# A modulated linear layer as the first stage of a long kernel, rebuilt as a pipeline over batches

## The reference

```
# first operation, per batch b (y = cond_1024, 8 x 256; weight 256 x 256)
w = scale * weight[:, :, :, 0] * y[:, None, :]
dnorm = rsqrt(sum(w * w, axis=2, keepdims=True) + 1e-08)
w = w * dnorm
E = Efou.reshape(b, in_f, img_size)
x = einsum('boi,bil->bol', w, E).reshape(b, img_size, out_f)
# second operation, the part concerned
qkv = x @ qkv_w
q_l = q.reshape(b, h, m, l, dh).mean(axis=3)      # m = 64 landmarks of l = 8 tokens
k_l = k.reshape(b, h, m, l, dh).mean(axis=3)
attn2 = softmax(q_l @ k_l^T) ; attn2_inv = six Newton iterations (pseudo-inverse)
```

## Time and profile before

| | us |
|---|---|
| median of the runs | 4001.85 |
| profiled execution, its own time | 3965.16 |
| its span, first to last instruction | 3963.4 |
| first matmul of `nystrom_stage` in it | 82.63 |
| mean granted TensorE clock | 0.746 of full |
| busy share: PE, DVE, ACT, POOL | 83%, 57%, 43%, 30% |

### The profile page before, as it was taken

The page is one execution under the profiler, slowest core; times in us unless marked ns, Lnnn a source line. Parts: engine busy times, 40 slices in busy tenths (PEclk is TensorE's granted clock), DMA queues, the critical chain, the costliest instruction groups (busy, mean ns, idle before and its releaser), DMA issues. The chain is left out here.

```text
span 3963.4 us, 142208 instructions
## 1 busy us (share of the span) xinstructions
PE 3296.6 (83%) x58228; PEld 2450.2 (62%) x58228; DVE 2267.9 (57%) x6676; ACT 1694.8 (43%) x5249; POOL 1201.1 (30%) x1587
## 2 busy tenths in 40 slices
PE   5667759898888888559984899999999979999682
PEld 4455448888888888535531466666666647777561
DVE  4437754444444444368865777877779755555333
ACT  0129633333333333247742455655556534444231
POOL 0012330000000000023320555554555554444432
PEclk8789955555555555589997899999999975555686
DMA  3001010000000000011101000000000010101335
GB/s 119 8 26 54 19 42 24 14 14 24 14 24 14 24 14 24 5 33 24 24 0 49 2 2 2 2 2 2 2 2 2 2 45 31 35 31 35 87 118 170
DMA packets 111064, 115.69 MB, mean 29 GB/s; under 512 B 53132, under 2 KB 94549, under 8 KB 110458
## 3 DMA queue, kind: packets, MB, share of 16 engines
q1 hardware_dynamic: 102762, 87.07, 7.8%
q0 software_dynamic: 7824, 21.46, 1.5%
HBM read 79.49 MB, written 29.00 MB: 27 GB/s over the span
## 5 line engine op out<-in xcount | busy, mean ns | idle before, releaser
L649 PE MATMUL banks<-hp,whp 128*128 128x8 f16 x24576 | 741.3, 168 | 117.5 <-DVE hp L716 117.5
L649 PEld LDWEIGHTS banks<-hp,whp 128*128 128x128 f16 x24576 | 697.7, 104 | 178.3 <-DVE hp L716 169.4
L682 ACT ACTIVATE ig<-banks 128x32 f32<-128x32 f32 x512 | 101.2, 198 | 577.5 <-PE banks L649 577.5
L1043 ACT ACTIVATE att_PH<-att_stp 128x1024 f16<-128x1024 f32 (+3 forms) x258 | 183.4, 711 | 374.0 <-PE att_stp L861 374.0
L711 DVE SCALAR_TENSOR_TENSOR carry<-ig 128x16 f32<-128x16 f32 x512 | 92.2, 180 | 425.3 <-ACT ig L682 425.3
L619 POOL COPY HT<-hist 128x128 f32 x64 | 21.2, 406 | 986.6 <-DVE hp L721 986.6
L1659 PEld LDWEIGHTS rnn_banks<-rnn_hp,rnn_whp 128*128 128x128 f16 x6144 | 251.8, 108 | 102.3 <-ACT rnn_hp L1717 70.9
L1659 PE MATMUL rnn_banks<-rnn_hp,rnn_whp 128*128 128x8 f16 x6144 | 285.5, 171 | 35.3 <-ACT rnn_hp L1717 11.2
L1108 POOL TENSOR_TENSOR att_QK<-att_rot,att_QK 128x512 f16<-128x512 f32 x133 | 173.6, 1305 | 338.5 <-ACT att_QK L1035 338.5
L627 PE MATMUL banks<-xs,wxp 128*128 128x64 f16 x3168 | 264.9, 241 | 0.0
L979 DVE TENSOR_TENSOR att_PL<-att_P,att_PH 128x1024 f16<-128x1024 f32 (+3 forms) x257 | 235.1, 934 | 18.1 <-ACT att_P L1049 16.5
(11 more groups left out here) (572 smaller groups left out, 7910.8 us busy)
## 6 DMA issues: line engine op xcount, KB each, us to landing
gen_w<-in_L_cond_W_dram SPq DMA_DIRECT2D x32, 512.0 KB, 4.2
exp_xt<-expert_rows_scratch SPq DMA_DIRECT2D x80, 129.0 KB, 2.3
edge_cb<-cols_scratch SPq DMA_DIRECT2D x16, 512.0 KB, 3.7
XT<-expert_found_scratch SPq DMA_DIRECT2D x16, 512.0 KB, 5.1
mod_xn<-in_x_dram SPq DMA_DIRECT2D x8, 512.0 KB, 3.7
XT<-in_xT_dram SPq DMA_DIRECT2D x1, 4096.0 KB
out_dram<-exp_ob SPq DMA_DIRECT2D x64, 64.0 KB, 2.2
attw_st<-in_L_attn_w_qkvT_dram SPq DMA_DIRECT2D x6, 512.0 KB, 4.4
```

What stands on the lines that cost most here:

```text
L649: last=nc.tensor.matmul(out, whp[:,wpart,k,col:col+128], hp[:,k,hpart], start=False,stop=True,skip_group_check=True)
L1043: nc.scalar.activation(PH[:,:,at:at+w_],st_ps[:,:,0:w_],ACT.Exp,scale=DH**-0.5)
```

## The change

`dense_stage` gets four buffers for `xn`, three for `wy`, and two for `sq`, `ps_n`, `rt` and `dn`. Scaling and squaring move from VectorE to ScalarE (`Copy` with a scale, and `Square`), one batch ahead of the root. TensorE sums the squares of batch b+1 before it mixes batch b. VectorE takes the reciprocal of batch b, then sums the eight-token groups of batch b-1 (`landmarks`, two instructions of 512 columns), then writes `HT` of batch b. SyncE issues `XT` after the attention's weights instead of ahead of them. `nystrom_stage` loses its two long sums and TensorE's wait for them; `lm` is allocated outside of both stages, and the counts of the semaphore `dv` shift by one.

```diff
-def dense_stage(nc, XT, HT, x, xT, condT, wT_in, h0T, loads):
+def dense_stage(nc, XT, HT, x, xT, condT, wT_in, h0T, lm, loads):
 
     with ExitStack() as ctx:
         sb=lambda n,s,d=F32: ctx.enter_context(nc.sbuf_tensor("mod_"+n,s,d))
         sem=ctx.enter_context(semaphores(nc,"mod_"))
-        W=sb("W",[P,2,D]); xn=sb("xn",[P,2,2,2*D]); wy=sb("wy",[P,2,2,D]); sq=sb("sq",[P,2,D]); rt=sb("rt",[P,D]); dn=sb("dn",[P,D]); eps=sb("eps",[P,1]); ones=sb("ones",[P,P]); ysc=sb("ysc",[P,2,NB])
-        ps_n=ctx.enter_context(nc.psum_tensor("mod_ps_n",[P,512],F32)); ps_d=ctx.enter_context(nc.psum_tensor("mod_ps_d",[P,2,2,512],F32))
-        x_in=[sem(f"x_in{i}") for i in range(2)]; w_in,h_in,xt_in,rest_in,const,yscaled,modded,squared,summed,rooted,inverted,mixed,kept=[sem(n) for n in "w_in,h_in,xt_in,rest_in,const,yscaled,modded,squared,summed,rooted,inverted,mixed,kept".split(",")]
+        XB=4; WB=3
+        W=sb("W",[P,2,D]); xn=sb("xn",[P,XB,2,2*D]); wy=sb("wy",[P,WB,2,D]); sq=sb("sq",[P,2,2,D]); rt=sb("rt",[P,2,D]); dn=sb("dn",[P,2,D]); eps=sb("eps",[P,1]); ones=sb("ones",[P,P]); ysc=sb("ysc",[P,2,NB])
+        ps_n=ctx.enter_context(nc.psum_tensor("mod_ps_n",[P,2,512],F32)); ps_d=ctx.enter_context(nc.psum_tensor("mod_ps_d",[P,2,2,512],F32))
+        x_in=[sem(f"x_in{i}") for i in range(XB)]; w_in,h_in,xt_in,rest_in,const,yscaled,modded,squared,summed,rooted,inverted,mixed,kept,meaned=[sem(n) for n in "w_in,h_in,xt_in,rest_in,const,yscaled,modded,squared,summed,rooted,inverted,mixed,kept,meaned".split(",")]
         block=ctx.enter_context(nc.Block())
         @block.sync
         def _(sp):
@@ -71,10 +72,10 @@
             sp.dma_start(h0T[:,:,:],condT).then_inc(h_in,16)
             sp.dma_start(W[:,:,:],wT_in.rearrange("(k p) o -> p k o",p=P)).then_inc(w_in,16)
             for b in range(NB):
-                if b>=2: sp.wait_ge(mixed,b-1)
-                sp.dma_start(xn[:,b%2],x[b].rearrange("(k i h) f -> i k (h f)",k=2,h=2)).then_inc(x_in[b%2],16)
+                if b>=XB: sp.wait_ge(mixed,b-XB+1)
+                sp.dma_start(xn[:,b%XB],x[b].rearrange("(k i h) f -> i k (h f)",k=2,h=2)).then_inc(x_in[b%XB],16)
+            for dst,src in loads: sp.dma_start(dst,src).then_inc(rest_in,16)
             sp.dma_start(XT[:,:,:,:],xT).then_inc(xt_in,16)
-            for dst,src in loads: sp.dma_start(dst,src).then_inc(rest_in,16)
             sp.wait_ge(xt_in,16); sp.wait_ge(rest_in,16*len(loads))
         @block.gpsimd
         def _(pool):
@@ -82,45 +83,58 @@
             nc.gpsimd.memset(eps[:,:],1e-8).then_inc(const,1)
         @block.vector
         def _(dve):
-            dve.wait_ge(h_in,16); dve.wait_ge(w_in,16)
+            dve.wait_ge(h_in,16)
             nc.vector.tensor_scalar(ysc[:,:,:],h0T[:,:,:],D**-0.5,None,ALU.mult).then_inc(yscaled,1)
-            dve.wait_ge(yscaled,1)
+            def landmarks(b):
+                dve.wait_ge(kept,b+1)
+                for k in range(2): i=nc.vector.tensor_reduce(out=lm[:,k,b*LMK:(b+1)*LMK],in_=HT[:,k,b,:].rearrange("p (m g) -> p m g",g=GROUP),axis=X_AX,op=ALU.add)
+                i.then_inc(meaned,1)
             for b in range(NB):
-                if b>=2: dve.wait_ge(mixed,b-1)
-                for k in range(2): nc.vector.tensor_scalar(wy[:,b%2,k],W[:,k],ysc[:,k,b:b+1],None,ALU.mult).then_inc(modded,1)
-                dve.wait_ge(modded,2*b+2); dve.wait_ge(summed,b)
-                nc.vector.tensor_tensor(sq[:,:,:],wy[:,b%2],wy[:,b%2],ALU.mult).then_inc(squared,1)
                 dve.wait_ge(rooted,b+1)
-                nc.vector.reciprocal(dn[:,:],rt[:,:]).then_inc(inverted,1)
+                if b>=2: dve.wait_ge(kept,b-1)
+                nc.vector.reciprocal(dn[:,b%2],rt[:,b%2]).then_inc(inverted,1)
+                if b: landmarks(b-1)
                 dve.wait_ge(mixed,b+1); dve.wait_ge(inverted,b+1)
                 for k in range(2):
                     for h in range(2):
-                        i=nc.vector.tensor_tensor(HT[:,k,b,h:T:2],ps_d[:,b%2,k,h*D:(h+1)*D],dn[:,:],ALU.mult)
+                        i=nc.vector.tensor_tensor(HT[:,k,b,h:T:2],ps_d[:,b%2,k,h*D:(h+1)*D],dn[:,b%2],ALU.mult)
                 i.then_inc(kept,1)
+            landmarks(NB-1)
         @block.scalar
         def _(act):
-            act.wait_ge(const,2)
+            act.wait_ge(const,2); act.wait_ge(yscaled,1); act.wait_ge(w_in,16)
+            def modulate(b):
+                if b>=WB: act.wait_ge(mixed,b-WB+1)
+                for k in range(2): nc.scalar.activation(wy[:,b%WB,k],W[:,k],ACT.Copy,scale=ysc[:,k,b:b+1]).then_inc(modded,1)
+                act.wait_ge(modded,2*b+2)
+                if b>=2: act.wait_ge(summed,b-1)
+                nc.scalar.activation(sq[:,b%2],wy[:,b%WB],ACT.Square).then_inc(squared,1)
+            modulate(0)
             for b in range(NB):
+                if b+1<NB: modulate(b+1)
                 act.wait_ge(summed,b+1)
-                if b: act.wait_ge(inverted,b)
-                nc.scalar.activation(rt[:,:],ps_n[:,0:D],ACT.Sqrt,bias=eps[:,0:1]).then_inc(rooted,1)
+                if b>=2: act.wait_ge(inverted,b-1)
+                nc.scalar.activation(rt[:,b%2],ps_n[:,b%2,0:D],ACT.Sqrt,bias=eps[:,0:1]).then_inc(rooted,1)
         @block.tensor
         def _(pe):
             pe.wait_ge(const,2)
+            def sums(b):
+                pe.wait_ge(squared,b+1)
+                if b>=2: pe.wait_ge(rooted,b-1)
+                for k in range(2): i=nc.tensor.matmul(ps_n[:,b%2,0:D],ones[:,:],sq[:,b%2,k],start=(k==0),stop=(k==1))
+                i.then_inc(summed,1)
+            sums(0)
             for b in range(NB):
-                pe.wait_ge(squared,b+1)
-                if b: pe.wait_ge(rooted,b)
-                for k in range(2): i=nc.tensor.matmul(ps_n[:,0:D],ones[:,:],sq[:,k],start=(k==0),stop=(k==1))
-                i.then_inc(summed,1)
-                pe.wait_ge(x_in[b%2],16*(b//2+1))
+                if b+1<NB: sums(b+1)
+                pe.wait_ge(x_in[b%XB],16*(b//XB+1))
                 if b>=2: pe.wait_ge(kept,b-1)
                 for f in range(2):
                     for h in range(2):
-                        for k in range(2): i=nc.tensor.matmul(ps_d[:,b%2,f,h*D:(h+1)*D],xn[:,b%2,k,h*D+f*P:h*D+(f+1)*P],wy[:,b%2,k],start=(k==0),stop=(k==1))
+                        for k in range(2): i=nc.tensor.matmul(ps_d[:,b%2,f,h*D:(h+1)*D],xn[:,b%XB,k,h*D+f*P:h*D+(f+1)*P],wy[:,b%WB,k],start=(k==0),stop=(k==1))
                 i.then_inc(mixed,1)
 
 
...
-def nystrom_stage(nc, HT, wqkv, out_w, out_b, conv, xg, ident, taps_dram):
+def nystrom_stage(nc, HT, lm, wqkv, out_w, out_b, conv, xg, ident, taps_dram):
...
-            lm=sb1("mean",[P,2,NB*LMK]); qbd=sb1("qbd",[P,LP,NB,P]); kl=sb1("kl",[P,LP,NB*LMK]); klbd=sb1("klbd",[P,LP,P])
+            qbd=sb1("qbd",[P,LP,NB,P]); kl=sb1("kl",[P,LP,NB*LMK]); klbd=sb1("klbd",[P,LP,P])
...
-                for k in range(2): i=nc.vector.tensor_reduce(out=lm[:,k,:],in_=HT[:,k,:,:].rearrange("p b (m g) -> p (b m) g",g=GROUP),axis=X_AX,op=ALU.add)
-                step(i)
...
-                pe.wait_ge(dv,1)
                 proj(A,0,[lm[:,k,:] for k in range(2)])
...
-            wqkv=sb0("lm_wqkv",[P,2,3*LI]); out_w=sb0("lm_out_w",[P,LP,D]); out_b=sb0("lm_out_b",[P,2]); xg=sb0("xg",[P,2,T])
+            wqkv=sb0("lm_wqkv",[P,2,3*LI]); out_w=sb0("lm_out_w",[P,LP,D]); out_b=sb0("lm_out_b",[P,2]); xg=sb0("xg",[P,2,T]); lm=sb0("lm_mean",[P,2,NB*LMK])
```

More of the change, by code:

```diff
@@ L220, in _ @@
                 nc.scalar.activation(v[:,:,:],A[:,:,:],ACT.Copy).then_inc(ac,1)
-                act.wait_ge(dv,5)
+                act.wait_ge(dv,4)
                 nc.scalar.activation(A2[:,:,:],A2[:,:,:],ACT.Exp).then_inc(ac,1)
-                act.wait_ge(dv,10)
+                act.wait_ge(dv,9)
                 nc.scalar.activation(A1[:,:,:],A1[:,:,:],ACT.Exp).then_inc(ac,1)
-                act.wait_ge(dv,15)
+                act.wait_ge(dv,14)
                 for j in range(LP): i=nc.scalar.activation(A3[:,j],B[:,j],ACT.Exp,bias=mx[:,2,j,1:2],accum_out=mx[:,2,j,2:3])
@@ L240, in _ @@
                 pe.wait_ge(ac,1); proj(A,0,tok)
-                pe.wait_ge(dv,2); proj(B,1,tok)
+                pe.wait_ge(dv,1); proj(B,1,tok)
                 pe.wait_ge(ac,2)
@@ L245, in _ @@
                 i.then_inc(st,1)
-                pe.wait_ge(dv,3)
+                pe.wait_ge(dv,2)
                 for j in range(LP):
@@ L253, in _ @@
                 i.then_inc(st,1)
-                pe.wait_ge(dv,5)
+                pe.wait_ge(dv,4)
                 for j in range(LP): i=nc.tensor.matmul(B[:,j,:],qbd[:,j,0],kT[:,j],start=True,stop=True)
                 i.then_inc(st,1)
-                pe.wait_ge(dv,14); pe.wait_ge(ac,6); pe.wait_ge(const,7)
+                pe.wait_ge(dv,13); pe.wait_ge(ac,6); pe.wait_ge(const,7)
                 for j in range(LP): i=nc.tensor.matmul(B[:,j,:],bd[:,:],A2[:,j],start=True,stop=True)
@@ L262, in _ @@
                 i.then_inc(st,1)
-                pe.wait_ge(dv,17)
```

(11 more changed lines are left out.)

## The result

The changed kernel takes 3968.61 us (median of four runs, 3965.36 to 3971.23), the kernel before 4002.04 beside it: ratio 0.9914, 95% interval 0.9897 to 0.9931, or 33.4 us less. A second comparison on another chip gave 3962.16 against 3998.87: 0.9906 (0.9891 to 0.9922).

A forecast was written before the change was run, and what follows sets the result against it. A chain of TensorE and VectorE taking turns bounds the first stage. Batches 23.6, XT 2.0, boundary 0.8, long sums 8.8, start -2.1, last sums -1.25 save 31.8 us: 4001.85 to 3970, forecast 3966 to 3974, range 3962 to 3979.

The forecast's parts named there:

- XT no longer the end: First stage's end: the load of XT stops ending the stage, saving 2.0 us.
- The start: First stage up to HT of batch 0: done at 17.4 instead of 15.3, costing 2.1 us.
- A batch: Middle of the first stage: 4.45 us a batch, both heavy engines wanting 4.4 to 4.45; 23.6 us saved over seven.
- rival 2: First stage: batches do not close up, 5.5 us each, 7.4 less saved, 3977.4 us; chance 0.13.
- The end of the stage: First stage's end: VectorE's last sums end at 49.8, boundary 1.0, next stage starts at 50.8.
- XT is late by nothing, with 1.6 to spare: First stage's end: XT lands at 47.45, 18.1 us after the last x tile's issue, allowing a start at 49.2.
- rival 1: First stage's end: XT ends it after all, load 22 us, start 53.1, total 3972.3 us; chance 0.10.
- a landing after 50: First stage's end: a load landing later than 50 us was listed as showing the prediction wrong.
- The worth of ScalarE: First stage: scaling and squares kept on VectorE would add 1.3 us, making 5.75 a batch.
- The clock: Second stage and behind: 1.8 us more saved if the first projection's clock stays up; plus or minus 4 from slow steps.
- Rival 4: Long attention stretch, 1010 us: shift loses the 2.4 GHz clock for part; 100 us at low level gives 4020; chance 0.03.
- The median: Whole kernel: median 36.7 us above the profiled execution; saving of 31.8 taken over unchanged, 4001.85 to 3970.

The follow-up runs named there:

- one and two batches ahead: Changed kernel with scaling and squares back on VectorE, one or two batches ahead: ratio to the kernel before 0.9962 with one, 0.9916 with two.
- the sums alone: Kernel before with only the eight-token sums moved into its first stage, long sums gone: 3958.0 us against 3967.7, ratio 0.9970.
- the shift: Changed kernel with seven unused sums of 4096 columns on VectorE at the first stage's end: 3996.2 us against 3998.6, ratio 0.9995.
- the second trace of before: Kernel before, no edit, run and traced once more: median 3999.9 us against 3998.6, ratio 1.0002, traced span 3996.1.

## Why the prediction was right

The forecast was 3970, the result 3968.61. The mechanism is the one named in its two large parts: the chain through both engines opened, and the long sums went off the path. The runs with one and two batches ahead, the sums alone and the shift show it. The small part, "XT no longer the end", came out otherwise. And how close the median came is luck in part: the second stage came 30.85 sooner where 31.8 was forecast, the medians differ by 33.4, and that difference is known to some 7 us only (ratio 0.9897 to 0.9931). Term by term:

- **The start.** First squares at 8.55 (forecast 8.7), two scalings 0.91 (0.94), square 0.63 (0.65). The sums of two batches ended at 12.44, not 11.5, and the first mixing took 4.81, not 4.45; HT at 17.09, not 16.0. In the seven traces with this start the first HT is at 15.88 to 17.09. The scaling begins at 6.98, 0.01 after the table load's end. The drain of 1.38 us that the Trainium skill (ScalarE: Activation LUTs, What ACT_TABLE_LOAD costs) adds to a switch of table is not seen here either.
- **A batch.** 4.29 on average (30.02 for seven), not 4.45. TensorE sets it, with no gap, and not VectorE, whose 4.34 and 0.1 for handovers were taken too large: where TensorE has less to do, VectorE goes from HT to HT in 4.12. By luck this made good the 1.1 of the start: VectorE's last sum ends at 49.83, forecast 49.8. No slow batch came, as expected, and rival 2 (5.5 a batch) is out.
- **The end of the stage.** This is the step that failed: "XT is late by nothing, with 1.6 to spare". XT did end the stage; rival 1 came true in kind and cost 0.9, and so did the prediction's own sign of being wrong, a landing after 50 (50.81). From the issue of the last x tile to the last packet it was 20.3 us, not 18.1. I had called "the bytes and the queue" the same, and passed over the turned order: XT is now issued 2.05 behind the last x tile (32.08 and 30.03) and was issued 0.41 behind it before, since three transfers stand between. From XT's own issue to the last packet it is 18.3 after 17.8. The reading behind it was wrong too: before, it was the weights behind XT that landed last, at 72.84, and XT had been there since 67.39. The boundary was 1.9 instead of 1.0, the second stage at 51.78 instead of 50.8.
- **The worth of ScalarE.** I had put 5.75 a batch on VectorE without it; it was 5.33, and the whole move is worth 1.0 us at the second stage, since the later start and the late boundary cost most of what the batches save. The Trainium skill's rule to multiply on VectorE (ScalarE: Activation LUTs, Rules for kernel authors) holds per instruction, 0.52 against 0.91 for two scalings; by the time of the kernel the two places are alike.
- **The clock.** No saving at the first projection; 3.0 lost in the pseudo-inverse, within the 4 allowed. Rival 4 did not come: over the 1010 us from 2190 on the granted clock is 1.00 and TensorE busy for 999.02. Against the second trace of before the change is 27.6 ahead at the end of the pseudo-inverse's stage (240.62 and 268.25) and 35.3 at the last recurrence (3204.1 and 3239.4). Two traces of the kernel before itself differ by 5.6 between these places, so where the 2 to 6 us beyond the first stage's 31 come from, if they are there at all, is not settled.
- **The median.** 36.7 above the trace of before was taken over as it was. It came from the longer kind of recurrence and last stage. The traced runs among the timed ones (the change here, the kernel before in the run above) are of that kind, so it was most likely in both medians and cancels.

## What to carry to other kernels

When two engines are each busy for half of a loop and their times add up to it, look for the instruction that closes the circle and move it far enough ahead that nothing waits for it: two batches on the fullest engine here, one on an idle one. Which engine executes it matters far less. Before trusting a gain at the end of a stage, find which transfer lands last, and add it up from its own issue, with all that the change puts in front of it. And when the profiled execution and the timed runs disagree, trace the kernel before a second time before explaining it by the change.

## What was not expected of the hardware

In one kind of execution SyncE's register, move and assert instructions of the last stage take 0.70 us at times, where they take at most 0.16 in the other, and the stage is 18 to 25 us longer; the same program comes in both. And a stretch in which TensorE takes turns with VectorE took 91.6 to 98.1 us for the same instructions, at a mean granted clock of 0.87 to 0.80: a few us saved ahead of it can be gone behind it, or come out as more.
